# Differential and masked attention with mixtures of experts on one core: a third context buffer and two key chunks per step in layer 1, a new order of the matrix work in layer 0

## The reference, cut to what matters

```python
def _L0_xattn_ref(query, key_, value, Wq, Wk, Wv, Wp, bp, ...):     # H = 16, HD = 4
    q = (query @ Wq.T).reshape(B, Nq, 2 * H, HD).transpose(0, 2, 1, 3)
    k = (key_ @ Wk.T).reshape(B, Nk, 2 * H, HD).transpose(0, 2, 1, 3)
    v = (value @ Wv.T).reshape(B, Nk, H, 2 * HD).transpose(0, 2, 1, 3)
    attn = _sdpa(q1, k1, v) - lam * _sdpa(q2, k2, v)                # softmax of each
    ...                                                             # norm per head, @ Wp.T + bp
def _L1_xattn_ref(query, key, value, mask, ...):                    # 16 heads of 8
    scores = jnp.einsum('bhqd,bhkd->bhqk', q, k) / jnp.sqrt(jnp.float32(HD))
    scores = jnp.where(mask[:, None, :, :], jnp.finfo(scores.dtype).min, scores)
    ctx = jnp.einsum('bhqk,bhkd->bhqd', jax.nn.softmax(scores, axis=-1), v)
    ...
x = x + jnp.tanh(g_xattn[0]) * _L0_xattn_ref(_layernorm(x), ctx_1024, ctx_1024, ...)
x = x + jnp.tanh(g_ffn[0]) * _L0_ffn_ref(_layernorm(x), ...)
x = x + jnp.tanh(g_xattn[1]) * _L1_xattn_ref(_layernorm(x), ctx_1024, ctx_1024, mask, ...)
x = x + jnp.tanh(g_ffn[1]) * _L1_ffn_ref(_layernorm(x), ...)
```

## Time and profile before

| | us |
|---|---|
| median of 3 runs | 2349.78 (2349.38 to 2350.72) |
| the profiled execution | 2345.43 |
| its span, first to last instruction | 2343.1 |
| PE busy | 2179.4 (93%) |
| DVE, ACT, POOL busy | 1677.4, 1507.4, 1278.7 |
| mean granted TensorE clock | 0.953 of 2.4 GHz |

### The profile page before, as it was taken

The page is one execution under the profiler, slowest core; times in us unless marked ns, Lnnn a source line. Parts: engine busy times, 40 slices in busy tenths (PEclk is TensorE's granted clock), DMA queues, the critical chain, the costliest instruction groups (busy, mean ns, idle before and its releaser), DMA issues. The chain is left out here.

```text
span 2343.1 us, 67447 instructions
## 1 busy us (share of the span) xinstructions
PE 2179.4 (93%) x27256; PEld 1297.5 (55%) x27256; DVE 1677.4 (72%) x3701; ACT 1507.4 (64%) x2133; POOL 1278.7 (55%) x1418
## 2 busy tenths in 40 slices
PE   3799999999999999999976967999999999999798
PEld 2255555555555555555535853666665666666576
DVE  3688888888888888888825455777776677775644
ACT  2177787787787787787773322677676667667322
POOL 5335555555655655655423445677776777772332
PEclk9599999999999999999997985999999999999799
DMA  3635344344344344344201018576665666661100
GB/s 102 130 75 117 89 100 115 89 103 114 88 103 113 94 100 111 97 98 110 48 2 64 24 35 158 126 143 148 137 140 128 136 137 138 146 124 36 55 1 16
DMA packets 95245, 227.82 MB, mean 97 GB/s; under 512 B 46308, under 2 KB 58852, under 8 KB 88292
## 3 DMA queue, kind: packets, MB, share of 16 engines
q1 hardware_dynamic: 94692, 223.67, 42.3%
q10 hardware_dynamic: 256, 0.00, 0.0%
HBM read 146.77 MB, written 76.48 MB: 95 GB/s over the span
## 5 line engine op out<-in xcount | busy, mean ns | idle before, releaser
L1075 ACT ACTIVATE probs<-score_ps 125x896 f32<-125x896 f32 x1152 | 1014.2, 915 | 203.3 <-PE score_ps L968 200.9
L1133 DVE TENSOR_REDUCE max_part<-max_ps 112x1 f32<-112x500 f32 x1024 | 654.3, 668 | 115.2 <-PE spare_ps L937 66.9
L984 PE MATMUL acc_ps<-probs,vext 125*32 125x224 f32 (+1 forms) x12288 | 670.7, 316 | 2.7 <-issue 2.1
L937 PE MATMUL max_ps<-kstack,qstack 48*112 48x500 f16 x1535 | 507.1, 405 | 4.7 <-DVE max_part L1133 2.6
L968 PE MATMUL score_ps<-qstack,kstack 50*125 50x224 f16 (+1 forms) x6144 | 453.6, 243 | 15.7 <-ACT probs L1075 13.9
L968 PEld LDWEIGHTS score_ps<-qstack,kstack 50*125 50x125 f16 x6144 | 343.1, 134 | 181.1 <-issue 120.2
L1130 DVE CUSTOM_DVE_ANT_0 kstack<-max_ps,kstack 112x500 f32<-112x500 f32 x511 | 335.2, 675 | 127.1 <-PE max_ps L937 75.0
L1133 DVE TENSOR_REDUCE max_part<-spare_ps 112x1 f32<-112x500 f32 x512 | 343.1, 670 | 64.3 <-PE max_ps L937 64.3
L984 PEld LDWEIGHTS acc_ps<-probs,vext 125*32 125x32 f32 x12288 | 260.8, 109 | 220.1 <-issue 151.0
L937 PE MATMUL spare_ps<-kstack,qstack 48*112 48x500 f16 x769 | 310.0, 403 | 19.2 <-issue 15.8
L937 PEld LDWEIGHTS max_ps<-kstack,qstack 48*112 48x112 f16 x1535 | 173.2, 128 | 142.7 <-issue 77.7
(11 more groups left out here) (200 smaller groups left out, 2688.3 us busy)
## 6 DMA issues: line engine op xcount, KB each, us to landing
kstack<-k_parts SPq DMA_DIRECT2D x384, 187.5 KB, 6.6
k_parts<-khl SPq DMA_DIRECT2D x128, 375.0 KB, 2.7
ctx_f<-in_ctx SPq DMA_DIRECT2D x32, 750.0 KB
ctx_f<-context_parts SPq DMA_DIRECT2D x32, 750.0 KB, 4.5
context_parts<-ctx_f SPq DMA_DIRECT2D x16, 750.0 KB, 3.7
context_parts<-kstack SPq DMA_DIRECT2D x16, 750.0 KB, 3.5
mask_in<-in_mask SPq DMA_DIRECT2D x128, 82.0 KB
qrows<-q_parts SPq DMA_DIRECT2D x384, 7.0 KB, 7.0
```

Of the source, the lines that this page charges most:

```text
L937: nc.tensor.matmul(room(("P", n, p))[0:PIECE, 0:TK], qstack[n % SLOTS][rows, c, PIECE * i:PIECE * (i + 1)], kstack[n % SLOTS][rows, c, TK ...
L984: last = nc.tensor.matmul(acc_ps[32 * j:32 * j + 32, TT * S * i:TT * S * (i + 1)].rearrange("p (s c) -> p s c", s=S), vext[n % SLOTS][:, t ...
L1075: nc.scalar.activation(probs[t % 2][:, 896 * h:896 * h + 896].rearrange("k (b c) -> k b c", b=2), score_ps[(t * H + h) % 2][0:KT, :, 0:448 ...
L1133: nc.vector.reduce_max(best, scores, AX.X).then_inc(s_red, 1)
```

## The change

Layer 1 goes over 6 steps of two key chunks each, with the two chunks' scores in the two score buffers and their exponentials in the two halves of a `probs` buffer (`STEPS`, `chunk`). Its preparations move to new steps and into score banks, the output is turned in one piece (`uses_f`), search of n+2 starts at step 3 of 6. Its context parts get a third buffer in `XnT`; their load waits for the values of one element earlier, and SP issues it behind the maxima instead of ahead of them. POOL converts the search's mask first. In layer 0 the buffers and steps stay, and the order inside a step changes: `order_of` picks it by what this step and the one before prepare. In full loops that is "both scores first" in step 1, "apart by half the product" in steps 2 to 5, "apart by the product" in steps 0 and 6 to 11. In layer 1 it is "both scores first" in steps 0 and 1, "by the product" in 2 to 4, "by a pair" in 5.

```diff
-        self.uses_f = 2
+        self.uses_f = self.halves
+        self.steps = NKT if self.halves == 2 else NKT // 2
 
 
...
-    return T["ctx_f"][:, i, 0:SK].bitcast(F16).rearrange("p (a k) -> p a k", a=2)
+    room = T["XnT"][:, 0:SK] if i == 2 else T["ctx_f"][:, i, 0:SK]
+    return room.bitcast(F16).rearrange("p (a k) -> p a k", a=2)
 
 
 def load_context(sp, T, L, n):
 
     loaded = T[L.name + "_context_loaded"]
     if L.masked:
-        sp.dma_start(context_parts(T, n % 2), T["ctx_dram"][n:n + 1, :, :, :].rearrange("b d a k -> (b d) a k")).then_inc(loaded[n % 2], 16)
+        sp.dma_start(context_parts(T, n % 3), T["ctx_dram"][n:n + 1, :, :, :].rearrange("b d a k -> (b d) a k")).then_inc(loaded[n % 3], 16)
     else:
         sp.dma_start(T["ctx_f"][0:KT, 1, :].rearrange("p (t d) -> p t d", t=NKT),
...
+    ctxT = [context_parts(T, i) for i in range(3)] if L.masked else [
+        context_parts(T, 0), T["kstack"][2][:, K_WORDS:K_WORDS + 2 * SK].rearrange("p (a k) -> p a k", a=2)]
+    CTX = len(ctxT)
     context_f = T["kstack"][0][:, K_WORDS:K_WORDS + 2 * SK].bitcast(F32)
     qstack = [T["qstack"][i][:, 0:PAIRS * GC].rearrange("p (c q) -> p c q", c=PAIRS) for i in range(SLOTS)]
...
     if L is L0:
-        where = {("T", 0): (1, 1), ("F", 0): (2, 1), ("T", 1): (3, 1), ("F", 1): (4, 1), ("T", 2): (5, 1), ("K", 0): (6, 1),
-                 ("M", 0): (7, 1), ("V", 0): (7, 1), ("K", 1): (8, 1), ("V", 1): (9, 1), ("K", 2): (10, 1), ("A", 0): (11, 1),
-                 ("V", 2): (11, 1)}
+        where = {("T", 0): (1, 0), ("F", 0): (2, 0), ("T", 1): (3, 0), ("F", 1): (4, 0), ("T", 2): (5, 0), ("K", 0): (6, 0),
+                 ("M", 0): (7, 1), ("V", 0): (7, 0), ("K", 1): (8, 0), ("V", 1): (9, 0), ("K", 2): (10, 0), ("A", 0): (11, 1),
+                 ("V", 2): (11, 0)}
...
     else:
-        where = {("V", 0): (0, 2), ("F", 0): (1, 2), ("V", 1): (2, 2), ("F", 1): (3, 2), ("V", 2): (4, 2), ("K", 0): (5, 2),
-                 ("K", 1): (6, 2), ("M", 0): (7, 2), ("K", 2): (8, 2), ("A", 0): (10, 2)}
+        where = {("F", 0): (1, 1), ("K", 0): (1, 0), ("K", 1): (2, 0), ("K", 2): (2, 1), ("M", 0): (3, 1), ("V", 0): (3, 0),
+                 ("V", 1): (4, 0), ("V", 2): (4, 1), ("A", 0): (5, 1)}
...
-    per_step = L.pieces // NKT
-    assert per_step * NKT == L.pieces
-    AHEAD = 5
+    per_step = L.pieces // STEPS
+    assert per_step * STEPS == L.pieces
+    AHEAD = 3 if L.masked else 5
     early = AHEAD * per_step
+    ORDERS = {"both scores first": ("scores 0", "scores 1", "pair 0", "weigh", "pair 1", "prepare"),
+              "scores apart by a pair": ("scores 0", "pair 0", "scores 1", "weigh", "pair 1", "prepare"),
+              "scores apart by the product": ("scores 0", "pair 0", "weigh", "scores 1", "pair 1", "prepare"),
+              "scores apart by half the product": ("scores 0", "pair 0", "weigh 0", "scores 1", "weigh 1", "pair 1", "prepare"),
+              "pairs apart by preparation": ("scores 0", "weigh", "scores 1", "pair 0", "prepare", "pair 1")}
+
+    def order_of(n, t):
+        if not L.masked and any(kind in "TF" for kind, _, _ in at_step(n, t)) and at_step(n, t - 1):
+            return ORDERS["scores apart by half the product"]
+
+        busy = [any(kind not in "AM" for kind, _, _ in at_step(*place)) for place in ((n, t), (n, t - 1) if t else (n - 1, STEPS - 1))]
+        if not busy[1]:
+            return ORDERS["both scores first"]
+        if L.masked and not busy[0]:
+            return ORDERS["scores apart by a pair"]
+        return ORDERS["scores apart by the product" if L.masked and busy[0] else "scores apart by the product" if busy[0] else "scores apart by the product"]
...
     order = [("P", 0, p) for p in range(L.pieces)] + [("M", 0, 0)] + [("P", 1, p) for p in range(early)]
     spare_uses, in_scores = list(first_preps) + [("M", 0, 0)], {}
     for n in range(B):
-        for t in range(NKT):
-            middle, last = at_step(n, t, 1), at_step(n, t, 2)
-            spare_uses += middle + last
-            if H == 2:
-                in_scores.update({user: n * NKT + t for user in middle})
-                middle = []
-            order += searched(n, t, 0) + middle + searched(n, t, 1) + last
+        for t in range(STEPS):
+            spare_uses += at_step(n, t)
+            in_scores.update({user: n * STEPS + t for user in at_step(n, t)})
+            order += searched(n, t, 0) + searched(n, t, 1)
...
                 if L.masked:
-                    at_least(sp, s_v, NTHIRD * (n - 1))
+                    at_least(sp, s_v, NTHIRD * (n - 2))
                 else:
                     sp.wait_ge(s_ctxT, NTHIRD * n)
...
                     load_mask(sp, T, L, n)
 
...
-                        next_context(n + 4)
                 if n + 3 < B and not L.masked:
                     next_context(n + 4)
                     store_context(n + 3)
                 if n + 1 < B:
                     fill_m(n + 1)
                 if n + 3 < B:
+                    if L.masked:
+                        next_context(n + 4)
                     store_k(n + 3)
 
...
+                    nc.gpsimd.tensor_scalar(by_chunk(mask_add[n % SLOTS]), turned_keys(T["mask_in2"][:, :]),
+                                            -BIG * BIG, None, ALU.mult).then_inc(s_add, 1)
                     nc.gpsimd.tensor_scalar(by_chunk(mask_f[n % SLOTS][0:HALF + SQ, :]), turned_keys(mask_in[0:HALF + SQ, :]),
                                             -BIG, None, ALU.mult).then_inc(s_big, 1)
-                    pool.wait_ge(s_big, n + 1)
-                    nc.gpsimd.tensor_scalar(by_chunk(mask_add[n % SLOTS]), turned_keys(T["mask_in2"][:, :]),
-                                            -BIG * BIG, None, ALU.mult).then_inc(s_add, 1)
 
             def split_context(n, i):
...
+                step = n * STEPS + t
+                number = step * 2 + place
                 h = halves_of(step)[place]
-                if L.masked:
-                    at_least(pe, s_exp, number - 1)
-                elif place == 0:
+                if place == 0:
                     at_least(pe, s_exp, number)
                 else:
                     at_least(pe, s_exp, number - 2)
...
-                buf = score_ps[(t * H + h) % 2]
-                keys = slice(KT * t, KT * t + KT)
+                buf = score_ps[h]
+                chunk, columns = (t, range(h * 2, h * 2 + 2)) if H == 2 else (2 * t + h, range(PAIRS))
+                keys = slice(KT * chunk, KT * chunk + KT)
...
+            def weigh(n, t, halves=(0, 1)):
+
+                if halves[0] == 0:
+                    pe.wait_ge(s_exp, (n * STEPS + t + 1) * 2)
+                if t == 0 and halves[0] == 0:
+                    at_least(pe, s_os, n)
+                    pe.wait_ge(s_v, NTHIRD * (n + 1))
+                chunks = [(t, 0)] if H == 2 else [(2 * t + h, 896 * h) for h in range(2)]
...
+                if halves[-1] == 1:
                     last.then_inc(s_av, 1)
...
             for n in range(B):
-                for t in range(NKT):
+                for t in range(STEPS):
                     weighed = (n, t - 1) if t else (n - 1, LAST)
-                    scores(n, t, 0)
-                    search(searched(n, t, 0))
-                    if H == 2:
-                        scores(n, t, 1)
-                    for i in range(2):
-                        if i == 1 and (t or H == 1):
-                            search(searched(n, t, 1))
-                            for user in at_step(n, t, 1):
+                    for work in order_of(n, t):
+                        if work in ("scores 0", "scores 1"):
+                            scores(n, t, int(work[-1]))
+                        elif work in ("pair 0", "pair 1"):
+                            search(searched(n, t, int(work[-1])))
+                        elif work[0:5] == "weigh" and weighed[0] >= 0:
+                            weigh(*weighed, (int(work[-1]),) if work[-1] in "01" else (0, 1))
+                        elif work == "prepare":
+                            for user in at_step(n, t):
                                 use(user)
-                        if weighed[0] >= 0:
-                            weigh(*weighed, i)
-                    if t == 0 and H == 2:
-                        search(searched(n, t, 1))
-                    for user in at_step(n, t, 2):
-                        use(user)
-            for i in range(2):
-                weigh(B - 1, LAST, i)
+            weigh(B - 1, LAST)
...
-                    if t == where["F", 1][0] + 1 and n:
+                    if t == where["F", L.uses_f - 1][0] + 1 and n:
```

More of the change, by code:

```diff
@@ L504, in attend @@
     layer = 0 if L is L0 else 1
-    GD, GC, H = L.group_dims, L.group_cols, L.halves
+    GD, GC, H, STEPS = L.group_dims, L.group_cols, L.halves, L.steps
     K_WORDS = PAIRS * SK
@@ L589, in attend, with at_step @@
     LEAD = {"T": 3, "K": 3, "V": 2, "M": 1, "F": -1, "A": -1}
-    def at_step(n, t, side):
```

(54 more changed lines are left out.)

54 lines of the change are left out of this document (25 added, 29 removed).

## The result

| | before | after |
|---|---|---|
| median of 3 runs, us | 2349.78 (2349.38 to 2350.72) | 2425.49 (2421.25 to 2428.61) |
| span of the profiled execution | 2343.1 | 2419.5 |
| PE busy | 2179.4 | 2122.1 |
| mean granted TensorE clock | 0.953 | 0.923 |

The ratio is 1.032 (1.0294 to 1.0346): the change makes the kernel 76 us slower, where 2329 was forecast. PE is busy for 57 us less, so the time is in waits. Two rows of the changed kernel's windows view say in which layer; they answer to the earlier trace rows. Columns: busy PE, PEld, DVE, ACT, POOL, then granted clock, share of the DMA engines, GB/s.

A forecast was written before the change was run, and what follows sets the result against it. PE was taken to bound the kernel, with ACT's chain setting some layer 0 steps and a DMA ring layer 1 after the change; layer 0's -12 and layer 1's -8 us took 2349.8 to 2329 (range 2288 to 2356).

The forecast's parts named there:

- Steps 6 to 11: Layer 0, steps with keys or values: ACT's chain sets 2.85 us against 2.99 and 3.08; with maxima and values 2.95.
- Step 1: Layer 0, both scores first: counted at 2.63 to 2.65 us on PE.
- Scores between the halves: Layer 0, steps 2 to 5: scores 1 between the product's halves cost 0.34 us, bounds 0.28 and 0.50.
- Steps 2 to 5: Layer 0, context and output steps: +0.14 us each on 2.8, so 2.95, with ACT's chain of 2.47 hidden.
- rival 4: Layer 0, steps 2 to 5: a mode change costs 0.25, the extra way out and in 0.50; kernel 2369; chance 0.04.
- 20.15: Layer 1: us per loop that PE and ACT alone need with six steps, against 22.3.
- a ring through SP's queue: Layer 1: key stack landing, search, maxima, context issue, key store and next fill close a ring of 22.3 us per loop.
- Landing of the store, "2.8, plus 1.4": Layer 1: key store lands 2.8 us after issue, plus 1.4 for the 750 KB context ahead; bounds 0 and 2.0.
- absorbs most of the scattered delays: Layer 1, step 3: PE's wait of about 2 us absorbs delays; 0.39 us gained per loop, 8 taken in all.
- Rival 2: Layer 1: store behind context load on SP lengthens the ring; 28 us per us, no gain from 22.98; 2361; chance 0.16.
- no waits of the product for ACT: Layer 1, sign: waits of the product for the exponential vanish; four made 1.16 us per loop.
- the context load every 22.2 us: Layer 1, sign of the loop time: the context load recurs every 22.2 us; over 23 would show rival 2.

The follow-up runs named there:

- store first: The changed kernel with the key store issued ahead of the context load on SP (maxima, key store, context): 2311.14 us, ratio 0.983 to the kernel before.
- context early: The changed kernel with the context load back right behind the mask on SP, third buffer kept: 2286.41 us, ratio 0.971 to the kernel before.
- busy wait: The changed kernel with layer 1's first scores of step 3 computed nine times for elements 1 to 29: 2409.52 us, ratio 1.0237 to the kernel before.

## Why the prediction was wrong

**Layer 0: right, and low by 8 us.** -12 forecast, -20 in the trace, -21 by the run with layer 0 alone. The rows of the changed kernel, a step with keys, step 1, an output step and a context step:

```profile
588.74 0.41 PE L981 MATMUL score_ps<-qstack,kstack 50*125 50x224 f16 x4
...
591.60 0.41 PE L981 MATMUL score_ps<-qstack,kstack 50*125 50x224 f16 x4
...
603.06 0.60 PE L981 MATMUL score_ps<-qstack,kstack 50*125 50x224 f16 x8 [0.80 <-ACT probs L1086]
...
605.62 0.41 PE L981 MATMUL score_ps<-qstack,kstack 50*125 50x224 f16 x4
...
606.74 0.41 PE L981 MATMUL score_ps<-qstack,kstack 50*125 50x224 f16 x4
607.08 0.59 PE L999 MATMUL acc_ps<-probs,vext 125*32 125x224 f32 x8
607.59 0.42 PE L952 MATMUL max_ps<-kstack,qstack 48*112 48x500 f16 x2
607.94 0.62 PE L936 MATMUL score_ps<-wide,out_sb 128*56 128x128 f32 x4
608.49 0.41 PE L981 MATMUL score_ps<-qstack,kstack 50*125 50x224 f16 x4
...
611.41 0.41 PE L981 MATMUL score_ps<-qstack,kstack 50*125 50x224 f16 x4
```

- Steps 6 to 11: 2.86 (588.74 to 591.60), forecast 2.85. That ACT's chain, absent before, takes over as the bound was right to 0.01. The step with maxima and values came to 2.88, not 2.95.
- Step 1: 2.56, forecast 2.64.
- Scores between the halves: 607.08 - 606.74 = 0.34, as forecast (bounds 0.28 and 0.50). Steps 2 to 5 are 2.87 to 2.92 rather than 2.95, because the pair behind the product takes 0.35 (607.59 to 607.94). The forecast read 0.47 in the earlier trace rows and took it all for the price of entering row-tiled work. Here both matmuls of the pair stand in one row at 607.59; in the earlier trace rows the pair is in two rows, and in the trace of before the second matmul starts 0.13 behind the first, at 605.97. That it waited there for its search bank fits, but was not tried by itself.
- The size: -0.74 a loop against -0.46 makes the 8 us.
- The rule of the Trainium skill ("TensorEngine Tiling (Array Packing)", Key Properties) that a mode change drains TensorE holds here as a price: scores between two halves of the product take 0.34 where they take 0.19 among their like, so one more way into row-tiled work and out of it is 0.15 us, and the forecast of rival 4 (0.50) is out. The half order buys nothing either, since ACT's chain gives 2.86 to 2.91 without it.

**Layer 1: the mechanism right, two of its terms too small, the sign wrong.** That PE and ACT alone need 20.15 was good (19.97 is the shortest loop). That a ring through SP's queue takes this back, its links and their order, was good too, and the links on SP and of the fill are right to 0.2. By the rival's own price, 28 us per us of ring, 3.75 more make 2329 + 105 = 2434, less the 8 of layer 0: 2426, and 2425.5 was measured. The steps that failed:

1. *Landing of the store, "2.8, plus 1.4".* It was 6.41: 2.2 too small, and outside the bounds of 0 to 2.0. I took from the two key stores that 750 KB pass in about 2 us. The windows view of the changed kernel between store and fill of the loop shown above has the rates. From 1901.70 to 1908.20 the context and both stores pass, 750 KB each. From 1902.10 to 1905.30 every packet is the context's, from 1906.00 nearly every one is the stores':

```profile
1902.10:1905.30 3.20, 3.19 (x69) 2.52 (x71) 1.80 (x5) 2.58 (x5) 1.72 (x2) 1.00 0.95 186
1906.00:1907.70 1.70, 1.70 (x48) 1.44 (x48) 1.70 (x7) 1.35 (x3) 1.70 (x1) 1.00 0.97 387
```

At 387 GB/s 750 KB take the 2 us of the forecast, but at 186 they take 4.1. From its first packet to its last the context passes in 4.2 us (median of 27 loads), and the store's first packet moves 3.8 us after its issue, where it was 0.9 in the kernel before. So the case that the forecast set as its upper bound is what happened, the store moving only once the context had passed, and the size of the context's passing was wrong: 2.2 more than 2.0, put into the forecast's own sum, make 2.8 + 1.4 + 2.2 = 6.4.

Part of this could be read before. The context loads of the kernel before (line 312), with nothing behind them, pass in 3.1 us; with that the forecast's ring would have been 23.4, over its break-even of 22.98. Why they need 4.2 with the stores behind them was not tried. The landing of those loads says it less plainly:

```profile
DMA to landing us min/median/max: 4.0/4.5/5.7
```

The 2.8 of the earlier trace rows is for one store, half as many bytes. At the stores' rate the other half would add 1.0, and the context would land in 3.8; it took 4.5.

The Trainium skill ("DMA: Bandwidth & Descriptors", Queues, rings and completion order) says that a DMA engine consumes descriptors in ring order; the trace agrees for the store behind the context (it lands in 6.6 against the context's 5.6, issued 0.49 later, so some 1.5 behind). With the store first, the context lies ahead of the fill, and the head of the fill waits for it as well. The fill's first DMA lands 3.8 us after its issue in the changed kernel and 5.9 with the store first (means over the loops; 4.0 and 6.1 in the two loops shown). But the other five DMAs then land within 6.1 us of the first instead of 7.4, so that of the 2.1 only 0.8 is left. Why they go faster is open.

2. *The clock, which has no term.* The forecast said that PE would wait about 2 us and that this wait "absorbs most of the scattered delays", as if a wait cost its length at most. The wait itself lengthens the next round: behind it the product takes 1.72 rather than 0.97, the maxima come 1.3 later (5.27 against 3.95), and everything on the ring moves with them. With 2.03 from the pair to the transpose, as at full clock, in place of 3.37 the link would be 3.93, which is the forecast's 3.95. Filling the wait with work brings the clock back (1.00 for 0.54) and 19 us of time. The two causes are not independent. In the two kernels with the store first or the context early, PE waits little, and the clock is lost for 7 and 10 us only.

**Which place on the queue.** Rival 2 named the right suspect, the store behind the context, and the forecast gave it 0.16. The ring's sums for the four orders:

| | after | store first | context early | busy wait |
|---|---|---|---|---|
| to maxima split | 5.27 | 4.38 | 4.37 | 4.74 |
| to store issued | 3.05 | 2.53 | 2.54 | 3.03 |
| store lands | 6.41 | 3.05 | 2.86 | 6.44 |
| fill lands | 11.28 | 12.04 | 11.27 | 11.38 |
| round | 26.0 | 22.0 | 21.0 | 25.6 |

Of the 5.0 us between the changed kernel and the best order, 3.55 are the store's landing, 0.5 the context's issue on SP, 0.9 the way to the split maxima, which is mostly the clock. Two further signs that the forecast named: no waits of the product for ACT came true (0.7 us in 600), the context load every 22.2 us did not (26.0).

## What to carry to other kernels

Once a loop's bound is a ring through a queue, never put a transfer that it doesn't need directly ahead of one that it does. Here exchanging the two turned 3.2% slower into 1.7% faster, and issuing the unneeded one earlier, while the queue was free, made it 2.9% faster; the extra buffer paid only where it let the load be issued early. Size such a transfer by the rate of its own kind in the trace, and not by that of another with as many bytes. And give every forecast wait of PE of some microseconds a second term for the clock, read from work behind a wait.

## What the runs showed of the hardware

- After 4.5 us without a matmul, the 4.9 us that follow ran at a granted clock of 0.54, though the 11 us before the pause and the 8 us after the 4.9 were at 1.00. Two different waits did it (on the key stack, 143 us at the lower level in layer 1; on the maxima, 133 us).
- The six DMAs of a fill move 1.15 MB in 11.2 us with the DMA engines busy for 0.91 to 1.01 of the time at 103 to 107 GB/s; with shares as high (0.95 and 0.97) the context load runs at 186 GB/s and the two stores at 387. A 750 KB load slipped in ahead of a fill costs it 0.8 us (2.1 at its first DMA); slipped in ahead of a store, which was to land in 2.9, it costs 3.5.
- The way into row-tiled work and out of it, between two halves of a product, costs 0.15 us.
